# Split units through three rotating in-place buffers, one more plain unit in layer 1, and the gram matrix as two bursts of 64-row matmuls

## The chip, the cores and the metric

One core of one Trainium2 chip. The metric is the device time of one execution in microseconds (us); the median of three runs of the kernel before is 1188.52 us (1185.98 to 1189.31). Engines in the rows: PE is TensorE, PEld its weight loads, DVE is VectorE, ACT is ScalarE, POOL is GpSimd, SP is SyncE, which issues nearly all DMAs.

## The reference: what is computed

For 512 samples, 64 embeddings of 16 floats are looked up in 64 tables. Three layers of a compressed interaction network follow, then a small dense net on their sums:

```
e = stack(tbl_f[ids[:, f]])                 # 512 x 64 x 16
x = e
for W, b in ((W0, b0), (W1, b1), (W2, b2)):
    z = einsum('bhd,bfd->bhfd', x, e).reshape(B, h * f, d)
    x = einsum('oc,bcd->bod', W, z) + b     # o = 128
    outs.append(x.sum(axis=2))
h = relu(relu(concat(outs, dense) @ W_top1 + b_top1) @ W_top2 + b_top2)
y = h @ W_top3
```

All is float32. Only the sum of layer 3 over d is needed, so the kernel computes it from the gram matrix of x2 and e: gram[h, f] = sum over d of x2[h, d] e[f, d], for each sample.

## The kernel before

The batch goes through in 16 chunks of 32 samples, a chunk being 512 columns (sample, d). Partitions hold rows h. Layer 1 of a chunk is one group of 16 row tiles of z, plus one for the squares; layer 2 is four groups. A group has four units of four tiles of 128x512, at positions 0 to 3.

A unit is formed by DVE as a product of a shifted copy of e (x0_shift) and a shifted copy of x, which ScalarE copies from `land` into a PSUM bank (`to_bank`, L779). Position 0 is plain fp32 (`float_unit`, L1037): TensorE multiplies it in two passes per tile. The three others are split into two parts in fp32r, z_hi (rounded by ScalarE, `round_unit`, L803) and z_lo (z minus z_hi), and each tile takes three matmuls with the likewise split weights (`split_tile`, L1042). For positions 1 and 3 the low part is made by GpSimd (`low_part`, L525); position 2 is formed in PSUM in two halves (`form_half`, L597) and split by DVE (`split_half`, L603). z, z_hi and z_lo have three slots of their own, one for each position; DVE's next unit of a position waits for GpSimd's subtraction of the one before, ScalarE's rounding for TensorE's use of the one before.

GpSimd also issues the gathers of the chunk after next, one or two after each low part, 16 per chunk (L516). Its round has ten low parts.

For the gram of the chunk before, x2 is turned (`turn_x2`, L1097), copied out as x2t (L838), and e is turned into x0t_ps (`turn_x0`, L1088). DVE makes from it four block matrices of eight samples each (`form_block`, L638), two buffers in turn: row (sample, d), columns (sample, field), zero off the sample's own block. `gram_of` (L1106) multiplies one: 128 rows, 512 columns, fp32, into turn_gram_ps; ScalarE copies it out (`take_gram`, L844), and only then may the next start. They are spread over a chunk: after position 0 of groups 1, 2 and 3 and at the end. SyncE stores the gram of each half chunk to HBM.

The order of each engine is written out by hand in its `round_`. TensorE's round is groups 0 and 1 of layer 2, layer 1 of the next chunk, groups 2 and 3. In the tail the 16 blocks of the gram are loaded from HBM (`load_gram`, L457) and multiplied with W2 (L1168, L1178); the dense net ends the kernel.

## Time and profile before

| | |
|---|---|
| runs, median (least to most) | 1188.52 us (1185.98 to 1189.31) |
| the profiled execution's own time | 1185.75 us |
| its span in the profile | 1183.9 us |
| TensorE clock granted, mean | 0.996 |
| HBM read, written | 114.96 MB, 27.53 MB |

A row of section 5 reads: line, engine, operation, written tile <- read tiles, shapes, count; then busy us and mean ns of one; then the engine's idle time just before, and what ended it. A row of a timeline reads: start in us, length in us, engine, line, operation, count, and in brackets the idle time before it with its releaser. TensorE's matmuls overlap in the records by their latency, so the distance of two starts says what one costs.

### The profile page before, as it was taken

How to read it: one execution, taken by the hardware profiler on the slowest of the kernel's cores; microseconds unless marked ns; L12 is line 12 of the kernel's file. 1: busy time of each engine (PE TensorE's matmuls, PEld its weight loads, DVE VectorE, ACT ScalarE, POOL GpSimd, SP SyncE). 2: the span in 40 equal slices, each digit the busy share in tenths (PEclk: the TensorE clock that was granted, in tenths of full speed). 3: DMA queues.
4: the chain of work that ended last, by engine and by line, in shares of the span. 5: the costliest groups of instructions: out<-in, count | busy, mean ns of one | idle time of the engine just before them, and what ended most of it. 6: DMA issues, size and time to landing. Idle time of an engine off the chain costs nothing.

```text
span 1183.9 us, 14016 instructions
## 1 busy us (share of the span) xinstructions
PE 1121.4 (95%) x4212; PEld 758.6 (64%) x4212; DVE 1013.0 (86%) x701; ACT 714.2 (60%) x712; POOL 981.2 (83%) x419
## 2 busy tenths in 40 slices
PE   0589999999999999999999999999999999999998
PEld 0346666666766666666667666666666676667685
DVE  4598899989899999999898989999998989996542
ACT  5365566666666666666666656666666666565633
POOL 6679999999999999999999999999999997776000
PEclk9989999999999999999999999999999999999999
DMA  6641414325262515143252525251432525242991
GB/s 239 185 125 54 113 47 143 98 79 157 70 167 73 145 59 166 46 129 110 78 155 71 166 73 148 58 163 46 132 107 78 156 71 165 73 152 107 276 297 48
DMA packets 103836, 142.86 MB, mean 121 GB/s; under 512 B 11745, under 2 KB 55009, under 8 KB 103042
## 3 DMA queue, kind: packets, MB, share of 16 engines
q1 hardware_dynamic: 95618, 140.42, 39.4%
q0 software_dynamic: 8192, 2.11, 2.1%
q8 instruction: 14, 0.23, 0.1%
q14 instruction: 12, 0.10, 0.0%
HBM read 114.96 MB, written 27.53 MB: 120 GB/s over the span
## 4 chain that ended last, share of the span: by engine, by line
POOL 62%; PE 18%; issue 15%; DMA 3%; DVE 1%; ACT 1%; SPq 0%; POOLq 0%; DVEq 0%; ACTq 0%
POOL z_lo L525 46%; POOL emb L516 16%; PE acc L1042 9%; PE acc L1037 4%; DMA z<-gram_scratch 2%; PE z_ps L1178 1%; PE turn_gram_ps L1106 1%; DMA land<-x_scratch 1%; PE z_ps L1168 1%; ACT z_hi L1004 0%; DVE z_lo L768 0%; DVE z L591 0%; PE turn_gram_ps L1210 0%; PE x0t_ps L1210 0%; DMA x_scratch<-emb 0%
## 5 line engine op out<-in xcount | busy, mean ns | idle before, releaser
L525 POOL TENSOR_TENSOR z_lo<-z,z_hi 128x2048 fp32r<-128x2048 f32 x159 | 735.1, 4623 | 47.2 <-ACT z_hi L803 44.6
L803 ACT ACTIVATE z_hi<-z 128x2048 fp32r<-128x2048 f32 x160 | 306.2, 1914 | 180.6 <-PE acc L1042 169.3
L1042 PE MATMUL acc<-z_hi,w_hi 128*128 128x512 f32 x960 | 412.2, 429 | 2.6 <-POOL z_lo L525 2.3
L1042 PE MATMUL acc<-z_hi,w_lo 128*128 128x512 f32 x960 | 378.8, 395 | 0.0
L1042 PE MATMUL acc<-z_lo,w_hi 128*128 128x512 f32 x960 | 378.8, 395 | 0.0
L591 DVE TENSOR_TENSOR z<-operand_even,x_shift 128x2048 f32<-128x2048 f32 x144 | 328.7, 2283 | 21.3 <-POOL z_lo L525 7.0
L516 POOL DMA_INDIRECT emb<-in_tables,rows_chunk x256 | 245.9, 961 | 61.9 <-issue 56.7
L1037 PE MATMUL acc<-z,w_sb 128*128 128x512 f32 x640 | 294.1, 603 | 0.5 <-ACT x L832 0.4
L603 DVE TENSOR_TENSOR z_lo<-z_ps,z_hi 128x1024 fp32r<-128x1024 f32 x160 | 194.8, 1218 | 72.3 <-ACT z_hi L812 72.3
L1042 PEld LDWEIGHTS acc<-z_hi,w_hi 128*128 128x128 f32 x960 | 180.7, 188 | 62.1 <-issue 18.4
L591 DVE TENSOR_TENSOR z<-operand_odd,x_shift 128x2048 f32<-128x2048 f32 x96 | 219.0, 2281 | 0.7 <-POOL z_lo L525 0.3
L1042 PEld LDWEIGHTS acc<-z_lo,w_hi 128*128 128x128 f32 x960 | 180.9, 188 | 57.2 <-issue 18.9
L1037 PEld LDWEIGHTS acc<-z,w_sb 128*128 128x128 f32 x640 | 121.6, 192 | 143.4 <-issue 127.2
L1042 PEld LDWEIGHTS acc<-z_hi,w_lo 128*128 128x128 f32 x960 | 180.7, 188 | 42.5
L812 ACT ACTIVATE z_hi<-z_ps 128x1024 fp32r<-128x1024 f32 x160 | 165.2, 1032 | 59.9 <-DVE z_ps L597 59.6
L597 DVE TENSOR_TENSOR z_ps<-operand_odd,x_shift 128x1024 f32<-128x1024 f32 x128 | 157.2, 1228 | 2.2
L779 ACT ACTIVATE operand_even<-land 128x512 f32<-128x512 f32 x96 | 57.4, 598 | 88.6 <-DMA land<-x_scratch 50.2
L844 ACT ACTIVATE gram<-turn_gram_ps 128x512 f32<-128x512 f32 x64 | 68.6, 1071 | 58.9 <-PE turn_gram_ps L1106 54.1
L1106 PE MATMUL turn_gram_ps<-blocks,x2t 128*128 128x512 f32 x128 | 67.8, 611 | 5.4 <-DVE blocks L638 5.3
L1065 PE MATMUL acc<-z_sq,w_sb 64*128 64x512 f32 x32 | 19.8, 701 | 47.1 <-ACT z_sq L818 39.9
L779 ACT ACTIVATE operand_odd<-land 128x512 f32<-128x512 f32 x96 | 57.2, 596 | 8.2 <-DMA land<-x_scratch 6.0
L638 DVE TENSOR_TENSOR blocks<-x0t_ps,mask_sb 128x512 f32<-128x512 f32 x64 | 43.6, 681 | 8.9 <-PE x0t_ps L1088 8.1
(106 smaller groups left out, 468.4 us busy)
## 6 DMA issues: line engine op xcount, KB each, us to landing
land<-x_scratch SPq DMA_DIRECT2D x128, 256.0 KB
land<-x_scratch SPq DMA_DIRECT2D x128, 128.0 KB
x_shift<-x_scratch SPq DMA_DIRECT2D x16, 1024.0 KB, 5.9
gram_scratch<-gram SPq DMA_DIRECT2D x32, 512.0 KB, 4.4
x_shift<-x_scratch SPq DMA_DIRECT2D x16, 768.0 KB, 8.0
z<-gram_scratch SPq DMA_DIRECT2D x10, 1024.0 KB, 10.8
x_scratch<-emb SPq DMA_DIRECT2D x32, 192.0 KB, 2.9
x_shift<-gram_scratch SPq DMA_DIRECT2D x6, 1024.0 KB, 10.5
```

The lines of the kernel that those rows point to most:

```text
L516: pool.indirect_dma_start(out=emb[:, c.par, j * EMBED:(j + 1) * EMBED], out_offset=None, in_=tables, in_offset=bass.IndirectOffsetOnAxis(a ...
L525: pool.tensor_tensor(z_lo[:, slot], z[:, Z_SLOT[pos]], z_hi[:, slot].bitcast(F32), ALU.subtract).then_inc(subtracted, 1)
L591: dve.tensor_tensor(z[:, Z_SLOT[pos]], *times(bank, QUAD, x0_tiles), ALU.mult).then_inc(formed, 1)
L597: dve.tensor_tensor(z_ps[:, :, :], *times(bank, 2, x0_tiles), ALU.mult).then_inc(halves_formed, 1)
L603: dve.tensor_tensor(z_lo[:, SPLIT_SLOT[2], tiles], z_ps[:, :, :], z_hi[:, SPLIT_SLOT[2], tiles].bitcast(F32), ALU.subtract).then_inc(halve ...
L779: act.activation(operand[bank][:, :], land[:, slot, :], ACT.Copy).then_inc(copied, 1)
L803: act.activation(z_hi[:, SPLIT_SLOT[pos]], z[:, Z_SLOT[pos]], ACT.Copy).then_inc(rounded, 1)
L812: act.activation(z_hi[:, SPLIT_SLOT[2], 2 * half:2 * half + 2], z_ps[:, :, :], ACT.Copy).then_inc(halves_rounded, 1)
L844: act.activation(gram[:, :, b % 2 * GROUP_B:(b % 2 + 1) * GROUP_B].rearrange("p f b -> p b f"), turn_gram_ps[:, :].rearrange("p (b f) -> p ...
L1037: mm = pe.matmul(acc[:, :], weights[:, tile0 + q, :], z[:, Z_SLOT[0], q, :], start=start and q == 0, stop=False)
L1042: mm = pe.matmul(acc[:, :], w[:, tile, :], zz[:, slot, q, :], start=False, stop=stop and n == 2)
L1106: pe.matmul(turn_gram_ps[:, :], x2t[:, b * P:(b + 1) * P], blocks[:, b % 2].rearrange("p b f -> p (b f)"), start=True, stop=True).then_inc ...
```

## The change

- Split units of positions 1 and 3 rotate through three buffers, z_hi slot and z_lo slot together; z lies in z_lo's memory, and GpSimd subtracts in place. Plain units rotate through two buffers z_float. `Group` gets functions that tell a unit's slot and which use of TensorE frees it; DVE's forming waits for that use. ScalarE's rounding waits for the formed unit alone.
- Layer 1's position 3 is a plain fp32 unit: no rounding, no low part; its weights move to w0_sb. GpSimd's round has nine low parts.
- The gram of a chunk is taken in two halves of two 128-row blocks. A block is two matmuls of 64 rows and 256 columns, one on partitions 0 to 63 into turn_gram_ps, one on 64 to 127 into x0t_ps's bank. The halves stand after position 0 of groups 1 and 2. One DVE instruction forms all blocks (128x1024), before the middle of group 1. ScalarE copies out both banks after each half, at other places of its round, the last after the rounding of the next chunk's first unit; TensorE waits for all four copies before the last unit of a chunk.
- The third piece of W2 is loaded two units later. The scratch for GpSimd's DMA descriptors is set to 8192.

The diff, cut to its core:

```diff
+HALF_ROWS = P // 2
+TILE_B = HALF_ROWS // EMBED
+HALVES, BANK_BLOCKS = 2, BLOCKS // 2
+GRAM_BANKS = 2
...
-L1_SPLIT = SPLIT_UNITS * QUAD
+L1_SPLIT = 2 * QUAD
 L2_SPLIT = L2_GROUPS * SPLIT_UNITS * QUAD
 SPLIT_TILES = L1_SPLIT + L2_SPLIT
-L1_PLAIN, L2_PLAIN = QUAD, L2_GROUPS * QUAD
-Z_SLOT = {0: 0, 1: 1, 3: 2}
-SPLIT_SLOT = {1: 0, 3: 1, 2: 2}
+L1_PLAIN, L2_PLAIN = 2 * QUAD, L2_GROUPS * QUAD
+FLOAT_SLOTS, UNIT_SLOTS = 2, 3
+HALVES_SLOT = UNIT_SLOTS
...
+    def layer1_at(self, back):
+        j = self.j - back
+        return j in (-1, 0) if self.chunk.is_(0) else self.has_layer1 and j == 2
+    def before(self):
+        if self.chunk.is_(0):
+            return 1 + self.j, min(1 + self.j, 2)
+        return 1 + self.j, 1 + (self.has_layer1 and self.j > 2)
+    def units(self, more=0):
+        groups, layer1 = self.before()
+        return self.chunk.count(2 * GROUPS - 1, 2 * groups - layer1 + more)
+    def unit_slot(self, pos):
+        groups, layer1 = self.before()
+        return (2 * groups - layer1 + pos // 3) % UNIT_SLOTS
+    def float_slot(self, pos):
+        groups, layer1 = self.before()
+        return (groups + layer1 + pos // 3) % FLOAT_SLOTS
+    def unit_freed(self, pos):
+        past = [(0, 1)] if pos == 3 else []
+        for back in range(1, 4):
+            past += [(back, 1)] if self.layer1_at(back) else [(back, 3), (back, 1)]
+        back, at = past[UNIT_SLOTS - 1]
+        return self.freed(back, at)
+    def float_freed(self, pos):
+        past = [(0, 0)] if pos == 3 else []
+        for back in range(1, 4):
+            past += [(back, 3), (back, 0)] if self.layer1_at(back) else [(back, 0)]
+        back, at = past[FLOAT_SLOTS - 1]
+        return self.freed(back, at)
+    def freed(self, back, at):
+        if self.chunk.is_(0) and self.j - back < -1:
+            return None
+        return self.count(QUAD, at + 1 - QUAD * back)
...
-        z = sb("z", [P, len(Z_SLOT), QUAD, COLS])
-        z_hi = sb("z_hi", [P, len(SPLIT_SLOT), QUAD, COLS], F32R)
-        z_lo, z_lo_whole = sb_twice("z_lo", "z_lo_whole", [P, len(SPLIT_SLOT), QUAD, COLS])
+        z_float = sb("z_float", [P, FLOAT_SLOTS, QUAD, COLS])
+        z_hi = sb("z_hi", [P, UNIT_SLOTS + 1, QUAD, COLS], F32R)
+        z_lo, z = sb_twice("z_lo", "z", [P, UNIT_SLOTS + 1, QUAD, COLS])
...
-        blocks = sb("blocks", [P, 2, GROUP_B, FIELDS])
+        blocks = sb("blocks", [P, BLOCKS, TILE_B, FIELDS])
...
+        gram_banks = [turn_gram_ps[:, :], x0t_ps[:, :, :].rearrange("p b f -> p (b f)")]
...
-            load_w2(3, 3)
+            load_w2(3, 3, units_used=2)
...
-                slot = SPLIT_SLOT[pos]
-                pool.wait_ge(rounded, g.count(2, (pos + 1) // 2))
-                pool.tensor_tensor(z_lo[:, slot], z[:, Z_SLOT[pos]], z_hi[:, slot].bitcast(F32),
+                slot = g.unit_slot(pos)
+                pool.wait_ge(rounded, g.units((pos + 1) // 2))
+                pool.tensor_tensor(z_lo[:, slot], z[:, slot], z_hi[:, slot].bitcast(F32),
                                    ALU.subtract).then_inc(subtracted, 1)
             def round_(c, look_up=True, groups=GROUPS):
                 done = 0
                 for j in range(groups):
                     for pos in (1, 3):
-                        low_part(Group(c, j), pos)
+                        if not (pos == 3 and Group(c, j).is_layer1):
+                            low_part(Group(c, j), pos)
...
-                if not g.is_first:
-                    if pos == 0:
-                        dve.wait_ge(used, g.count(4, -3))
-                    else:
-                        dve.wait_ge(subtracted, g.count(2, -2 + (pos + 1) // 2))
-                dve.tensor_tensor(z[:, Z_SLOT[pos]], *times(bank, QUAD, x0_tiles), ALU.mult).then_inc(formed, 1)
+                is_float = pos == 0 or pos == 3 and g.is_layer1
+                freed = g.float_freed(pos) if is_float else g.unit_freed(pos)
+                if freed is not None:
+                    dve.wait_ge(used, freed)
+                out = z_float[:, g.float_slot(pos)] if is_float else z[:, g.unit_slot(pos)]
+                dve.tensor_tensor(out, *times(bank, QUAD, x0_tiles), ALU.mult).then_inc(formed, 1)
...
-            def form_block(c, b):
-                if b == 0:
-                    dve.wait_ge(x0_turned, c.count(1, 1))
-                if not (c.is_(0) and b < 2):
-                    dve.wait_ge(gram_done, c.count(BLOCKS, b - 1))
+            def form_blocks(c):
+                dve.wait_ge(x0_turned, c.count(1, 1))
+                if not c.is_(0):
+                    dve.wait_ge(gram_done, c.count(HALVES))
+                shape = [P, BLOCKS, TILE_B, FIELDS]
                 dve.tensor_tensor(
-                    blocks[:, b % 2], x0t_ps[:, b:b + 1, :].to_broadcast([P, GROUP_B, FIELDS]),
-                    mask_sb[:, :].rearrange("p (b f) -> p b f", f=1).to_broadcast([P, GROUP_B, FIELDS]),
+                    blocks[:, :, :, :],
+                    x0t_ps[:, 0:BLOCKS, :].rearrange("p (k o) f -> p k o f", o=1).to_broadcast(shape),
+                    mask_sb[:, :].rearrange("p (k b f) -> p k b f", k=1, f=1).to_broadcast(shape),
                     ALU.mult).then_inc(block_ready, 1)
...
                 layer2(c, 1, 0)
+                form_blocks(prev)
                 layer2_middle(c, 1)
-                form_block(prev, 0)
                 layer1(nxt, 1)
                 split_half(layer2_group(c, 1), 1)
                 sum2(prev)
                 layer1(nxt, 0)
-                form_block(prev, 1)
                 layer1_middle(nxt)
-                form_block(prev, 2)
                 layer2(c, 2, 1)
...
             def round_unit(g, pos):
                 act.wait_ge(formed, g.count(3, pos))
-                if not g.is_first:
-                    act.wait_ge(used, g.count(4, pos - 3))
-                act.activation(z_hi[:, SPLIT_SLOT[pos]], z[:, Z_SLOT[pos]], ACT.Copy).then_inc(rounded, 1)
+                act.activation(z_hi[:, g.unit_slot(pos)], z[:, g.unit_slot(pos)], ACT.Copy).then_inc(rounded, 1)
...
-            def take_gram(c, b):
-                act.wait_ge(gram_done, c.count(BLOCKS, b + 1))
-                if b % 2 == 0 and not (c.is_(0) and b == 0):
-                    act.wait_ge(gram_stored, c.count(32, 16 * (b // 2)))
-                act.activation(gram[:, :, b % 2 * GROUP_B:(b % 2 + 1) * GROUP_B].rearrange("p f b -> p b f"),
-                               turn_gram_ps[:, :].rearrange("p (b f) -> p b f", f=FIELDS), ACT.Copy).then_inc(gram_staged, 1)
+            def take_gram(c, half, bank):
+                act.wait_ge(gram_done, c.count(HALVES, half + 1))
+                if bank == 0 and not (c.is_(0) and half == 0):
+                    act.wait_ge(gram_stored, c.count(32, 16 * half))
+                act.activation(gram[:, :, :].rearrange("p f (k r b) -> p r k b f", k=BANK_BLOCKS, r=GRAM_BANKS)[:, bank],
+                               gram_banks[bank].rearrange("p (k b f) -> p k b f", k=BANK_BLOCKS, f=FIELDS),
+                               ACT.Copy).then_inc(gram_staged, 1)
...
-                take_gram(prev, 2)
+                take_gram(prev, 1, 0)
                 round_half(e, 1)
                 to_bank(f, 1, 1, released_by_layer2(e, 1))
                 round_unit(f, 1)
+                take_gram(prev, 1, 1)
...
-            def float_unit(g, acc, weights, tile0, start=False):
-                pe.wait_ge(formed, g.count(3, 2))
+            def float_unit(g, acc, weights, tile0, pos=0, start=False, stop=False):
+                pe.wait_ge(formed, g.count(3, 2 if pos == 0 else 3))
                 for q in range(QUAD):
-                    mm = pe.matmul(acc[:, :], weights[:, tile0 + q, :], z[:, Z_SLOT[0], q, :], start=start and q == 0, stop=False)
+                    mm = pe.matmul(acc[:, :], weights[:, tile0 + q, :], z_float[:, g.float_slot(pos), q, :],
+                                   start=start and q == 0, stop=stop and q == QUAD - 1)
                 mm.then_inc(used, 1)
...
-                split_unit(g, 3, acc1, 2 * QUAD, stop=True)
+                float_unit(g, acc1, w0_sb, QUAD, pos=3, stop=True)
...
-                            pe.wait_ge(block_ready, c.count(BLOCKS))
+                            pe.wait_ge(gram_staged, c.count(BLOCKS))
...
-            def gram_of(c, b):
-                if b == 0:
+            def gram_of(c, half):
+                if half == 0:
                     pe.wait_ge(x2t_ready, c.count(1, 1))
+                    pe.wait_ge(block_ready, c.count(1, 1))
                 else:
-                    pe.wait_ge(gram_staged, c.count(BLOCKS, b))
-                pe.wait_ge(block_ready, c.count(BLOCKS, b + 1))
-                pe.matmul(turn_gram_ps[:, :], x2t[:, b * P:(b + 1) * P],
-                          blocks[:, b % 2].rearrange("p b f -> p (b f)"), start=True, stop=True).then_inc(gram_done, 1)
+                    pe.wait_ge(gram_staged, c.count(BLOCKS, GRAM_BANKS))
+                for k in range(BANK_BLOCKS):
+                    b = half * BANK_BLOCKS + k
+                    for r in range(GRAM_BANKS):
+                        rows = slice(r * HALF_ROWS, (r + 1) * HALF_ROWS)
+                        mm = pe.matmul(gram_banks[r][:, k * TILE_B * FIELDS:(k + 1) * TILE_B * FIELDS],
+                                       x2t[rows, b * P:(b + 1) * P],
+                                       blocks[rows, b].rearrange("p b f -> p (b f)"), start=True, stop=True)
+                mm.then_inc(gram_done, 1)
...
-                layer2(c, 3, (0,))
-                gram_of(prev, 2)
-                layer2(c, 3, (1, 2, 3))
+                layer2(c, 3, range(QUAD))
                 turn_x0(c)
-                gram_of(prev, 3)
...
-        "mask": (np.arange(P)[:, None] // EMBED == np.arange(GROUP_B)[None, :]).astype(np.float32),
+        "mask": (np.arange(P)[:, None] % HALF_ROWS // EMBED == np.arange(TILE_B)[None, :]).astype(np.float32),
...
-    nc = bacc.Bacc("TRN2", target_bir_lowering=False, num_devices=1)
+    nc = bacc.Bacc("TRN2", target_bir_lowering=False, num_devices=1, dynamic_dma_scratch_size=8192)
```

In ScalarE's round the other three copies stand after `round_unit(d, 1)`, after `take_x1(nxt)` and after `round_unit(e, 3)`.

## Rows read from the trace of the kernel before

**Rows 1.** The page, engines: busy us, share of the span, instructions.

```profile
PE 1121.4 (95%) x4212; PEld 758.6 (64%) x4212; DVE 1013.0 (86%) x701; ACT 714.2 (60%) x712; POOL 981.2 (83%) x419
```

**Rows 2.** The chain that ended last: shares by engine, then by line.

```profile
POOL 62%; PE 18%; issue 15%; DMA 3%; DVE 1%; ACT 1%; SPq 0%; POOLq 0%; DVEq 0%; ACTq 0%
POOL z_lo L525 46%; POOL emb L516 16%; PE acc L1042 9%; PE acc L1037 4%; DMA z<-gram_scratch 2%; PE z_ps L1178 1%; PE turn_gram_ps L1106 1%; DMA land<-x_scratch 1%; PE z_ps L1168 1%; ACT z_hi L1004 0%; DVE z_lo L768 0%; DVE z L591 0%; PE turn_gram_ps L1210 0%; PE x0t_ps L1210 0%; DMA x_scratch<-emb 0%
```

**Rows 3.** The chain piece by piece (start, us), and GpSimd's groups of section 5.

```profile
463.00 4.64 POOL z_lo L525
...
528.17 4.64 POOL z_lo L525
...
L525 POOL TENSOR_TENSOR z_lo<-z,z_hi 128x2048 fp32r<-128x2048 f32 x159 | 735.1, 4623 | 47.2 <-ACT z_hi L803 44.6
...
L516 POOL DMA_INDIRECT emb<-in_tables,rows_chunk x256 | 245.9, 961 | 61.9 <-issue 56.7
```

**Rows 4.** Waits from 131 to 910 us: us, times, longest.

```profile
PE turn_gram_ps L1106 <- DVE blocks L638: 4.7, 6, 1.4
...
POOL z_lo L525 <- ACT z_hi L803: 1.1, 2, 0.9
```

**Rows 5.** Timeline of ScalarE: start, us; one copy of x2 per chunk (chunks 0, 12, 13, 14).

```profile
131.30 0.69 ACT L832 ACTIVATE x<-acc,bias_sb 128x512 f32<-128x512 f32 x1 [2.22 <-PE acc L1042]
...
914.61 0.69 ACT L832 ACTIVATE x<-acc,bias_sb 128x512 f32<-128x512 f32 x1 [0.59 <-PE acc L1042]
...
980.20 0.69 ACT L832 ACTIVATE x<-acc,bias_sb 128x512 f32<-128x512 f32 x1 [0.67 <-PE acc L1042]
...
1044.93 0.69 ACT L832 ACTIVATE x<-acc,bias_sb 128x512 f32<-128x512 f32 x1 [0.74 <-PE acc L1042]
```

**Rows 6.** Busy us (and instructions) of each engine in a stretch, granted clock, DMA.

```profile
329.10:393.70 64.60, 64.60 (x239) 43.64 (x239) 59.87 (x42) 41.43 (x41) 61.00 (x27) 1.00 0.38 108
```

**Rows 7.** Timeline of TensorE in a steady chunk, and a unit from the chain.

```profile
485.04 0.39 PE L1042 MATMUL acc<-z_hi,w_lo 128*128 128x512 f32 x1
485.37 1.12 PE L1065 MATMUL acc<-z_sq,w_sb 64*128 64x512 f32 x2
486.42 3.70 PE L1037 MATMUL acc<-z,w_sb 128*128 128x512 f32 x8
...
498.35 3.59 PE L1037 MATMUL acc<-z,w_sb 128*128 128x512 f32 x8
501.79 1.02 PE L1106 MATMUL turn_gram_ps<-blocks,x2t 128*128 128x512 f32 x2
...
985.04 2.79 PE acc L1042 x12
```

**Rows 8.** Groups of section 5: DVE's block instruction and one of 1024 elements.

```profile
L597 DVE TENSOR_TENSOR z_ps<-operand_odd,x_shift 128x1024 f32<-128x1024 f32 x128 | 157.2, 1228 | 2.2
...
L638 DVE TENSOR_TENSOR blocks<-x0t_ps,mask_sb 128x512 f32<-128x512 f32 x64 | 43.6, 681 | 8.9 <-PE x0t_ps L1088 8.1
```

**Rows 9.** DVE, ScalarE's gram copy and TensorE about the end of a chunk.

```profile
514.45 2.28 DVE L591 TENSOR_TENSOR z<-operand_even,x_shift 128x2048 f32<-128x2048 f32 x1
...
L844 ACT ACTIVATE gram<-turn_gram_ps 128x512 f32<-128x512 f32 x64 | 68.6, 1071 | 58.9 <-PE turn_gram_ps L1106 54.1
...
520.87 0.39 PE L1042 MATMUL acc<-z_hi,w_hi 128*128 128x512 f32 x1
```

**Rows 10.** Timeline of TensorE at the start.

```profile
64.94 2.04 PE L1065 MATMUL acc<-z_sq,w_sb 64*128 64x512 f32 x2 [7.18 <-ACT x L825]
...
80.94 3.59 PE L1037 MATMUL acc<-z,w_sb 128*128 128x512 f32 x8
```

**Rows 11.** Tail: DMA issues on SyncE's queue, and ScalarE's last rounding of gram.

```profile
1087.30 0.43 SPq L474 DMA_DIRECT2D w_whole<-in_w  x1
...
1096.66 0.38 SPq L457 DMA_DIRECT2D z<-gram_scratch  x1
...
1161.08 1.91 ACT L1004 ACTIVATE z_hi<-z 128x2048 fp32r<-128x2048 f32 x1 [1.54 <-DMA z<-gram_scratch]
```

More of the change, by code:

```diff
@@ L129, in __init__ @@
         self.is_first = chunk.is_(0) and j == -1
+        self.has_layer1 = not chunk.is_(CHUNKS - 1)
+        self.is_layer1 = self.layer1_at(0)
     def count(self, per_group, more=0):
         return self.chunk.count(GROUPS * per_group, per_group * (1 + self.j) + more)
+    def layer1_at(self, back):
[30 more added lines that the diff above has]
+        return self.count(QUAD, at + 1 - QUAD * back)
     def copies(self, more=0):
@@ L232, in gram_view @@
             return b.rearrange("p q (h n) -> p (q h) n", h=CHUNKS // QUAD).rearrange("p c (f b) -> p c f b", f=F_BLOCK)
-        gram_buffers = [gram_view(b) for b in (z[:, 0], z[:, 1], z[:, 2], x0_shift[:, 1, 0:QUAD], x0_shift[:, 1, QUAD:])]
+        gram_buffers = [gram_view(b) for b in (z_float[:, 0], z_float[:, 1], z[:, HALVES_SLOT], x0_shift[:, 1, 0:QUAD], x0_shift[:, 1, QUAD:])]
         GRAM_BUFFERS = len(gram_buffers)
-        gram_hi, gram_lo = ([gram_view(b[:, slot]) for slot in range(len(SPLIT_SLOT))] for b in (z_hi, z_lo))
+        gram_hi, gram_lo = ([gram_view(b[:, slot]) for slot in range(UNIT_SLOTS)] for b in (z_hi, z_lo))
         GRAM_SLOTS = len(gram_hi)
         wt2_sb = land[:, 0:2, :].rearrange("p a (h n) -> p (a h) n", h=2)
-        h1, h2, y_sb = z[:, 2], z_lo_whole[:, 2], z_sq[0:1, :]
+        h1, h2, y_sb = z_float[:, 0], z_float[:, 1], z_sq[0:1, :]
         acc1 = ps("acc1", [P, COLS])
@@ L469, in reload_gram, with load_w2 @@
                 load_gram(k)
-            def load_w2(part, groups_used):
-                sp.wait_ge(used, Group(end, groups_used).count(4))
+            def load_w2(part, groups_used, units_used=0):
+                sp.wait_ge(used, Group(end, groups_used).count(4, units_used))
                 sp.dma_start(w2_parts[part], w2[:, part * W2_PART:(part + 1) * W2_PART, :]).then_inc(w2_in[part], 16)
@@ L542, in _ @@
                 gather(c, range(HALF_B))
-            low_part(layer1_group(Chunk(0, 0)), 3)
-            with pool.Fori(0, (CHUNKS - 2) // 2) as n:
-                round_(Chunk(n, 0))
-                round_(Chunk(n, 1))
+            round_(Chunk(0, 0))
+            round_(Chunk(0, 1))
+            with pool.Fori(0, (CHUNKS - 4) // 2) as n:
+                round_(Chunk(n, 2))
+                round_(Chunk(n, 3))
             round_(Chunk(0, CHUNKS - 2), look_up=False)
@@ L602, in split_half @@
                 tiles = slice(2 * half, 2 * half + 2)
-                dve.tensor_tensor(z_lo[:, SPLIT_SLOT[2], tiles], z_ps[:, :, :],
-                                  z_hi[:, SPLIT_SLOT[2], tiles].bitcast(F32), ALU.subtract).then_inc(halves_split, 1)
+                dve.tensor_tensor(z_lo[:, HALVES_SLOT, tiles], z_ps[:, :, :],
+                                  z_hi[:, HALVES_SLOT, tiles].bitcast(F32), ALU.subtract).then_inc(halves_split, 1)
             def layer1(c, pos, half=None):
@@ L759, in _ @@
             split_w2(1)
-            form_block(end, 2)
             split_w2(2)
-            form_block(end, 3)
             split_w2(3)
@@ L1045, in split_unit @@
             def split_unit(g, pos, acc, tile0, stop=False):
-                pe.wait_ge(subtracted, g.count(2, (pos + 1) // 2))
+                pe.wait_ge(subtracted, g.units((pos + 1) // 2))
                 for q in range(QUAD):
-                    mm = split_tile(acc, tile0 + q, SPLIT_SLOT[pos], q, stop and q == QUAD - 1)
+                    mm = split_tile(acc, tile0 + q, g.unit_slot(pos), q, stop and q == QUAD - 1)
                 mm.then_inc(used, 1)
```

61 lines of the change are left out of this document (24 added, 37 removed).

## Prediction

> **What bounds the kernel now.** The page comes first. TensorE (PE) is busy 95% of the span, GpSimd (POOL) 83%, VectorE (DVE) 86% [rows 1]: three engines near full, so shares decide nothing. The chain of waits says which ends last: 62% of it is POOL, two thirds of that z_lo, the subtraction that splits a unit, and PE is only 18% [rows 2]. The pieces of the chain in order of time show a round of POOL: z_lo starts at 463.00 and the same one of the next chunk at 528.17, 65.17 us later [rows 3]. It holds 10 z_lo at 4.62 us and 16 gathers at 0.96, together 61.6 us, and 3.6 us of gaps. From 131 to 910 us POOL waited for a rounded unit 1.1 us in all [rows 4]: it is full.
>
> How fast does the whole go? ScalarE's L832 takes x2 once per chunk. From 131.30 to 914.61 lie 12 chunks, so 65.28 us each, POOL's round and 0.1 [rows 5]. Later, 980.20 to 1044.93, POOL gathers no more and a chunk takes 64.73 us [rows 5]. One earlier chunk took 64.6, with PE busy 64.60 of 64.60 [rows 6]. So PE's own floor is 64.6, only 0.6 below POOL. Relief of POOL alone can't pay more than that; what the change does to PE decides.
>
> PE's floor from its own rows: 12 split matmuls, a unit, take 2.79 us, 0.2325 each; a plain fp32 unit (8 passes) is 498.35 to 501.79, 3.43 us; a gram block (2 passes) 0.86 us [rows 7]. 15 split units 41.9, 5 plain 17.2, 4 gram blocks 3.4, the squares with what surrounds them 1.15 (below): 63.6, and the two turns are the other 1.0.
>
> **The change part by part.** *Layer 1's fourth unit in plain fp32.* On POOL one z_lo of ten goes: 65.2 − 4.6 = 60.6 us a round. On ScalarE a rounding of 1.9 us goes, off the path (busy 41 of 65 us [rows 6]). On PE 12 split matmuls become 8 fp32 passes: 3.43 − 2.79 = +0.64 us a chunk, all on the path once PE bounds.
>
> *The gram on PE.* Four blocks, each 2 passes of 512 columns, become 8 matmuls of 64 rows and 256 columns, in two bursts of four. No row shows a pass of 256 fp32 columns over 64 rows; half of the 0.429 us pass is 0.2145. A burst has 8 such passes. Run one by one they take 1.72 us; wholly overlapped in pairs 0.86. In between: the two passes of one matmul use the same 64 rows and the same bank, so they can't overlap each other, and the queue holds them in order, pass 1 and 2 of the upper rows, then of the lower. Overlap then comes only between the second pass of one and the first of the next: slots A1, A2+B1, B2+C1, C2+D1, D2, five of 0.2145, 1.07 us. I take 1.07.
> Going over to 64 rows and back costs too: the squares are such a matmul. The last split one ends its slot at 485.04 + 0.23 = 485.27, the squares start at 485.37, use 0.86 and would be done at 486.23, the next unit starts at 486.42 [rows 7]: 0.10 + 0.19 = 0.29 us, for each burst.
> So a chunk's gram is 2 × (1.07 + 0.29) = 2.72 instead of 3.43: −0.71. Wholly overlapped 2.30 (−1.13), one by one 4.02 (+0.59).
> The Trainium skill (TensorEngine Tiling (Array Packing), Key Properties) says that tiles work in parallel, but that changing the tiling mode drains TensorE; the 0.29 us of the squares agrees with the drain. It also gives up to 2× for 64 rows; no run here shows that, and by a full 2× the gram would save 1.13 us a chunk, by none it would cost 0.59.
>
> *One block-matrix instruction on DVE.* Four of 0.68 us go [rows 8]. The new one writes 128x1024 from PSUM; the nearest is L597, also 1024 elements per partition, 1.23 us; upper end 4 × 0.68 = 2.72. I take 1.23. DVE's chunk is 59.9 us busy [rows 6], becomes about 59, and stays under PE. PE's wait for a block (4.7 us in all [rows 4]) goes: the instruction now comes ahead of the middle of group 1, while PE has 3.43 us of the plain unit to do. It hides itself.
>
> *Three in-place buffers.* DVE's form no longer waits for POOL's subtraction but for PE's use three units back, and ScalarE's rounding not for PE at all, which is off the path. Place by PE's clock, group start = 0, units at 0, 3.43, 6.22, 9.01, next group 11.8. Position 3 may be formed when position 1 of the group before is used, at −5.6; form 2.28, round 1.91, subtract 4.62 end at +3.3, needed at 9.01: 5.7 us to spare, about one more z_lo with a gather. Position 1 may be formed at −11.8 and has 6.4 to spare. Cost 0; without that cover PE waits by what is lacking. The subtraction in place has the same shape; I count it 0, and as POOL has 4 us of spare it could be 0.4 us dearer each before it bounds.
>
> *The moved waits.* x0t's bank now holds half of the gram, so PE's last split unit of a chunk (before turn_x0) waits for all four copies out, the last being after ScalarE's rounding of the next chunk's first unit. Queued behind that wait: PE's whole stream. By before's rows: the next chunk's first unit is formed at 514.45 + 2.28 = 516.73, rounded in 1.91 and the copy takes 1.07: 519.7. PE comes to its last unit at 520.87 [rows 9]: 1.2 us to spare, 0 on the path. Four copies of 1.07 us remain four.
>
> *Start.* PE's layer 1 of chunk 1 starts at 64.94, after a 7.18 wait [rows 10]: it comes from the 32 gathers and the loads behind them, which stay. From there to 131.30 [rows 5] are 66.3 us; floor of four layer 2 groups is 4 × 11.8, layer 1 took 16.0, to 80.94 [rows 10], together 63.2, so POOL costs 3.0 here, and 2 of its subtractions go: −3.0 + 0.64 = −2.4. The smaller descriptor scratch could make gathers wait: no row shows one that waited for its ring, the mean of all 256 is 0.96 [rows 3]; I take 0 and at most 3 us, as many in the start as make three of them twice as long.
>
> *Tail.* From 1098 on DMA bounds: 16 loads of gram (and 3 stores) fill the 63 us up to 1161, where the last rounding waits for its load [rows 11], and PE and ScalarE wait for them. Fewer PE steps there gain nothing. The third piece of W2 is loaded after two more units, about 1091 instead of 1087.30, still ahead of the first gram load at 1096.66 [rows 11]: 0, at most +3 if they collide.
>
> **Sum.** Period: 64.6 + 0.64 − 0.71 = 64.5, with 0.1 for small waits, as 64.73 stands to 64.6: 64.65. The 14 intervals from 131.30 to 1044.93 are 913.6; after 905.1: −8.5. Chunk 0: −2.4. Last interval, without layer 1: −0.7. Tail 0. Together −11.6: the span 1183.9 becomes 1172.3, the execution 1185.75 becomes 1174.1. The median of the runs shown is 1188.52, 2.8 above that execution; against it I predict 1177.
>
> **The rivals.**
> *Whole overlap (1171).* Pairs run side by side in both passes: 0.42 less a chunk, over 15 chunks −6 us. For: two banks, two row halves. Against: the order of the passes above.
> The Trainium skill (TensorE: Matmul & The Clock Gate, Measured speedup vs the span model) has 3.07 from four 32-row tiles, not 4; two at that efficiency would lie near this or the forecast.
> *No overlap (1196), the other side.* 64-row passes queue up. A chunk is 64.6 + 0.64 + 0.59 = 65.8, 0.55 over today and 1.3 over the forecast: +1.3 × 15 = 19 us. For: no row shows two matmuls at once, and in every row a pass starts a full slot after the last. Against: all these use the same rows of the array. It decides from a burst of about 1.4 us on: there the gram and the plain unit cost what POOL's relief gives.
> *PE doesn't reach its floor (1186).* The chain form, round, subtract is tied to PE's pace now, and POOL at 60.6 of 64.6 is 94% full; handovers keep the period near 65.2 while only the start gains. 14 × 0.6 over the forecast. For: today every chunk but some sits 0.7 above PE's floor. Against: 5.7 us of cover, and the chunk at 64.73 with similar chains.
> *The wait for four copies bites (1194).* If DVE is only just ahead of PE, the 1.2 us of cover goes and PE pays about 1.1 a chunk.
>
> **How the numbers follow.** Forecast 0.45, whole overlap 0.15, no overlap 0.17, floor missed 0.15, copies or gathers 0.08. What a measurement can tell from no change is 0.3%, 3.6 us. Faster: the first two and a quarter of the third kind, 0.64; same 0.12 (the floor missed); slower 0.24. The forecast's own range is 1171 to 1183. For 8 in 10: down to 1168, whole overlap with some of the switching hidden, up to 1194, so that only the no-overlap case stays out.
>
> **What would show it.** z_lo count 143 instead of 159 and POOL waiting for roundings in the middle; L832 64.5 to 64.8 apart; from float unit to split unit around a burst 1.36 us (1.15 with whole overlap, 2.0 with none); one blocks row of 1.23 us; no idle of PE ahead of a chunk's last split unit. Wrong it is if the burst is 1.7 or more, or if PE has idle stretches of a microsecond in each chunk.

## The result, and the profile after

The changed kernel takes 1183.31 us (median of 6 runs, 1182.75 to 1183.81); the kernel before took 1187.99 (6 runs, 1185.98 to 1189.31) beside it. The ratio of the times, after over before, is 0.9965 with a 95% interval of [0.9954, 0.9975]: faster by 4.2 us by the ratio and 4.7 by the two medians, where 11.6 were forecast. (Ratios here and below are those on record; they can differ from the quotient of the medians shown in the fourth place.) The profiled execution went from 1185.75 to 1183.49 us, its span from 1183.9 to 1181.5.

The page after answers to [rows 1 to 3] and [rows 8]. First the engines' busy time; then the chain that ended last, by engine and by line; then groups as line, engine, operation, tiles, count, busy us, mean ns, idle before and releaser.

```profile
PE 1117.9 (95%) x4276; PEld 745.3 (63%) x4276; DVE 997.4 (84%) x652; ACT 681.9 (58%) x695; POOL 905.2 (77%) x403
...
PE 83%; POOL 4%; issue 3%; DMA 3%; SPq 2%; ACT 2%; DVE 1%; ACTq 0%
...
L580 POOL TENSOR_TENSOR z_lo<-z,z_hi 128x2048 fp32r<-128x2048 f32 x143 | 659.5, 4613 | 116.8 <-ACT z_hi L849 110.3
L1079 PE MATMUL acc<-z_float,w_sb 128*128 128x512 f32 x768 | 349.1, 601 | 8.2 <-ACT x L878 7.6
```

GpSimd has left the chain (62% to 4%), TensorE is it (18% to 83%): the bound moved as the prediction had it. The subtraction costs no more in place: 4613 ns against 4623. The waits of the steady part, 131 to 910 us, answer to [rows 4]:

```profile
POOL z_lo L580 <- ACT z_hi L849: 46.0, 42, 2.5
...
PE acc L1079 <- ACT x L878: 6.3, 12, 0.6
```

GpSimd now waits 46 us instead of 1.1, and TensorE's granted clock is 1.00 in this stretch in both kernels, so the clock plays no part there. The last row is new: once in each chunk TensorE's first plain unit waits for ScalarE's copy of x2. It looks small. The timeline of TensorE shows what it is part of; start and length in us, the bracket is the idle time before:

```profile
500.99 0.48 PE L1153 MATMUL turn_gram_ps<-blocks,x2t 64*128 64x256 f32 x1
501.00 0.48 PE L1153 MATMUL x0t_ps<-blocks,x2t 64*128 64x256 f32 x1
501.31 0.38 PE L1153 MATMUL turn_gram_ps<-blocks,x2t 64*128 64x256 f32 x1
501.32 0.38 PE L1153 MATMUL x0t_ps<-blocks,x2t 64*128 64x256 f32 x1
...
501.75 0.38 PE L1153 MATMUL turn_gram_ps<-blocks,x2t 64*128 64x256 f32 x1
501.75 0.38 PE L1153 MATMUL x0t_ps<-blocks,x2t 64*128 64x256 f32 x1
502.06 0.50 PE L1085 MATMUL acc<-z_hi,w_hi 128*128 128x512 f32 x1
...
522.09 0.39 PE L1085 MATMUL acc<-z_hi,w_lo 128*128 128x512 f32 x1
522.41 0.46 PE L1131 MATMUL x0t_ps<-ident_sb,x_shift 64*128 64x64 f32 x4
523.34 3.69 PE L1079 MATMUL acc<-z_float,w_sb 128*128 128x512 f32 x8 [0.46 <-ACT x L878]
```

The same place in the kernel before, from its timeline:

```profile
523.42 0.40 PE L1042 MATMUL acc<-z_hi,w_lo 128*128 128x512 f32 x1
523.75 0.46 PE L1088 MATMUL x0t_ps<-ident_sb,x_shift 64*128 64x64 f32 x4
524.15 1.12 PE L1106 MATMUL turn_gram_ps<-blocks,x2t 128*128 128x512 f32 x2
525.11 3.60 PE L1037 MATMUL acc<-z,w_sb 128*128 128x512 f32 x8
```

The next plain unit reuses the bank of x2, so it can't start until ScalarE has copied x2 out, which needs the last split matmul to end. Before, turn and gram block filled that time: from the block's end (524.15 + 0.86 = 525.01) the unit starts 0.1 later. The turn alone leaves a hole. The slot of a matmul is the distance from its start to the next one's in an unbroken row, 0.23 us for a split one. The slot of the last split matmul ends at 522.09 + 0.23 = 522.32, the plain unit starts at 523.34, 1.02 later, and its record is 0.1 longer (3.69 against 3.60): 1.12 in all. Before, that stretch without the gram block was 525.11 − 0.86 − (523.42 + 0.23) = 0.60. So 0.52 us of every chunk came back.

The burst itself beat the forecast. In both passes the two halves start 0.01 us apart. A pair comes each 0.21 us, four pairs are 0.86, and 0.40 is lost going in and out (0.09 before the first pair, 0.10 more than a slot from the first pair to the second, 0.10 behind the last, 0.10 more than a slot from the first split matmul to the second): 1.26 us against 1.36 forecast, 2.52 a chunk against 3.43 before. The gram gave −0.91, not −0.71.

ScalarE's copies of x2 give the pace (chunks 0, 12, 13, 14, 15), as [rows 5]:

```profile
132.23 0.69 ACT L878 ACTIVATE x<-acc,bias_sb 128x512 f32<-128x512 f32 x1 [4.04 <-PE acc L1085]
...
912.90 0.69 ACT L878 ACTIVATE x<-acc,bias_sb 128x512 f32<-128x512 f32 x1 [3.16 <-PE acc L1085]
977.90 0.69 ACT L878 ACTIVATE x<-acc,bias_sb 128x512 f32<-128x512 f32 x1 [3.10 <-PE acc L1085]
1042.83 0.69 ACT L878 ACTIVATE x<-acc,bias_sb 128x512 f32<-128x512 f32 x1 [3.10 <-PE acc L1085]
1094.08 0.69 ACT L878 ACTIVATE x<-acc,bias_sb 128x512 f32<-128x512 f32 x1 [10.37 <-PE acc L1085]
```

Between the two profiled executions the span balances: the first copy came 0.9 us later, the 14 intervals shrank from 913.6 to 910.6 (−3.0), the last one from 51.7 to 51.25 (−0.4), what lies behind it grew by 0.1: −2.4. That the medians differ by 4.7 is more than that, because the profiled execution of the kernel before was 2.2 us quicker than its median; what its other executions spend there no trace shows.

### The profile page after: what moved, and what is told of

The parts are those of the page before. It is cut to its first block, busy times and chain, and to the rows that moved or that the text cites. A ratio compares the mean times of both kernels' runs of the same rounds, so it can differ in the third digit from the quotient of the medians.

```text
span 1181.5 us, 13928 instructions
## 1 busy us (share of the span) xinstructions
PE 1117.9 (95%) x4276; PEld 745.3 (63%) x4276; DVE 997.4 (84%) x652; ACT 681.9 (58%) x695; POOL 905.2 (77%) x403
## 4 chain that ended last, share of the span: by engine, by line
PE 83%; POOL 4%; issue 3%; DMA 3%; SPq 2%; ACT 2%; DVE 1%; ACTq 0%
PE acc L1085 50%; PE acc L1079 26%; POOL z_lo L580 3%; PE turn_gram_ps L1153 3%; DMA z_float<-gram_scratch 2%; PE acc L1108 1%; POOL emb L571 1%; ACT x L878 1%; DMA z<-gram_scratch 1%; PE z_ps L1214 1%; PE turn_gram_ps L1140 1%; DMA land<-x_scratch 1%; ACT z_hi L1046 0%; DVE z_lo L816 0%; SPq L512 0%
## 5 line engine op out<-in xcount | busy, mean ns | idle before, releaser
L580 POOL TENSOR_TENSOR z_lo<-z,z_hi 128x2048 fp32r<-128x2048 f32 x143 | 659.5, 4613 | 116.8 <-ACT z_hi L849 110.3
L1085 PE MATMUL acc<-z_hi,w_hi 128*128 128x512 f32 x896 | 379.0, 423 | 6.8 <-DVE z_lo L659 4.2
L1079 PE MATMUL acc<-z_float,w_sb 128*128 128x512 f32 x768 | 349.1, 601 | 8.2 <-ACT x L878 7.6
L1085 PE MATMUL acc<-z_lo,w_hi 128*128 128x512 f32 x896 | 354.3, 395 | 0.0
L849 ACT ACTIVATE z_hi<-z 128x2048 fp32r<-128x2048 f32 x144 | 275.1, 1910 | 53.6 <-DVE z L647 53.6
L1079 PEld LDWEIGHTS acc<-z_float,w_sb 128*128 128x128 f32 x768 | 144.4, 191 | 174.6 <-issue 166.4
L647 DVE TENSOR_TENSOR z<-operand_even,x_shift 128x2048 f32<-128x2048 f32 x80 | 183.0, 2287 | 37.3 <-PE acc L1085 16.6
L647 DVE TENSOR_TENSOR z_float<-operand_even,x_shift 128x2048 f32<-128x2048 f32 x64 | 146.1, 2283 | 10.2 <-PE acc L1079 8.6
L647 DVE TENSOR_TENSOR z<-operand_odd,x_shift 128x2048 f32<-128x2048 f32 x64 | 146.2, 2284 | 4.3 <-PE acc L1085 4.3
L647 DVE TENSOR_TENSOR z_float<-operand_odd,x_shift 128x2048 f32<-128x2048 f32 x32 | 73.0, 2282 | 5.0 <-ACT operand_odd L827 5.0
```

What stands on the lines that cost most here:

```text
L580: pool.tensor_tensor(z_lo[:, slot], z[:, slot], z_hi[:, slot].bitcast(F32), ALU.subtract).then_inc(subtracted, 1)
L647: dve.tensor_tensor(out, *times(bank, QUAD, x0_tiles), ALU.mult).then_inc(formed, 1)
L849: act.activation(z_hi[:, g.unit_slot(pos)], z[:, g.unit_slot(pos)], ACT.Copy).then_inc(rounded, 1)
L1079: mm = pe.matmul(acc[:, :], weights[:, tile0 + q, :], z_float[:, g.float_slot(pos), q, :], start=start and q == 0, stop=stop and q == QUAD ...
L1085: mm = pe.matmul(acc[:, :], w[:, tile, :], zz[:, slot, q, :], start=False, stop=stop and n == 2)
```

## The experiments

The theory put to test: the gram's gain is real and whole; TensorE is the bound; the removed gram block had covered the copy of x2. Each variant's time is set against the kernel before on its own chip; a copy of x2 per chunk gives the pace.

**e1: is the wait slack?** The turn of e is issued twice, more work in the hole.

```diff
-                turn_x0(c)
+                turn_x0(c, times=2)
```

> The changed kernel with turn_x0's four transposes issued twice, so that TensorE has 0.4 us more work between the last split unit of a chunk and the next chunk's plain unit. Theory (there TensorE waits about 0.5 us for ScalarE's copy of x2, which the last gram matmul used to cover): the transposes fill the wait, the distance of two x2 copies stays within 0.1 us of 65.04 and the time within 2 us of 1183.3. Rival (the whole of TensorE's work sets the time, the wait is a product of how the records are read): 16 times 0.4 us more, about 1189.5.

Ratio 0.9964 [0.9950, 0.9978], 1182.01 us against 1185.86. Four matmuls more per chunk cost nothing, the copies of x2 stay 65.05 us apart (65.04):

```profile
519.33 0.71 PE L1131 MATMUL x0t_ps<-ident_sb,x_shift 64*128 64x64 f32 x8
520.25 3.69 PE L1079 MATMUL acc<-z_float,w_sb 128*128 128x512 f32 x8 [0.21 <-ACT x L878]
```

The matmuls run longer (0.71 against 0.46) and the idle time shrinks by the same 0.25. The hole is there and its end is set by ScalarE.

**e2: fill the hole with work that must be done anyway.** The second burst goes to the end of the chunk, the turn of e behind the turn of x2 in the next; ScalarE's copies of that half move with them.

```diff
-                layer2(c, 2, (0,))
-                gram_of(prev, 1)
-                layer2(c, 2, (1, 2, 3))
+                layer2(c, 2, range(QUAD))
                 layer2(c, 3, range(QUAD))
-                turn_x0(c)
+                gram_of(prev, 1)
```

> The changed kernel with its second gram burst moved from position 0 of group 2 to the end of the chunk, turn_x0 moved behind turn_x2 of the next round, and ScalarE's copies moved accordingly (its rounding of position 3 ahead of the copy of x2). Theory (uncovered x2 copy): a burst of 1.26 us now covers the 1.02 us from the last matmul to x2's release; the end of a chunk and both turns cost 0.5 us less, the x2 copies come 64.5 us apart, the time is 8 us under the changed kernel, about 1175.5. Rival (another unit is late as soon as this wait goes: GpSimd at 60.6 us a round or DVE near 59 with handovers): no gain, 1182 to 1185, with PE waiting for z_lo or formed units.

1175.1 us, ratio 0.9907 [0.9892, 0.9922]. Copies of x2 from 129.99 to 1032.85 over 14 intervals, 64.49 apart against 65.04: −0.55, the 0.52 of the hole. From 131 to 910 us TensorE's wait for the copy is nearly gone, one case where the changed kernel had twelve (6.3 us):

```profile
PE acc L1081 <- ACT x L878: 0.8, 1, 0.8
```

The theory holds. Against the changed kernel's profile the span is 6.5 us shorter: −7.7 from the 14 intervals, −2.2 from a first copy that comes earlier (the start, e3 and e11, which this edit doesn't touch), and +3.3 from the last interval, 54.58 instead of 51.25 (e10).

**e3: is the smaller descriptor scratch the cause of the late start?** The kernel before with it alone.

```diff
-    nc = bacc.Bacc("TRN2", target_bir_lowering=False, num_devices=1)
+    nc = bacc.Bacc("TRN2", target_bir_lowering=False, num_devices=1, dynamic_dma_scratch_size=8192)
```

> The kernel before with one edit, the descriptor scratch at 8192. Theory (the start's 3 us come from the smaller scratch, which slows the issue of DMAs): layer 1 of chunk 1 begins about 2 us later, near 67, the time is 2 us up. Rival (the start is later for another reason, such as where weights land): starts at 64.9, time unchanged within 0.5 us.

1185.15 us, ratio 0.9995 [0.9986, 1.0004]; layer 1 of chunk 1 starts at 65.66 (64.94 before, 67.06 after), and SyncE's loads are issued as early as in the kernel before (by 41.1 us; e11). The smaller scratch alone doesn't make the late issue, and e6 has the late issue without it.

**e4: does the overlap need the two halves as neighbours in the queue?** All matmuls of the upper rows first, then those of the lower.

```diff
-                for k in range(BANK_BLOCKS):
-                    b = half * BANK_BLOCKS + k
-                    for r in range(GRAM_BANKS):
+                for r in range(GRAM_BANKS):
+                    for k in range(BANK_BLOCKS):
+                        b = half * BANK_BLOCKS + k
```

> The changed kernel with the four matmuls of a gram burst in another order: both blocks of partitions 0 to 63 first, then both of 64 to 127, instead of alternating. Theory (neighbours overlap only if they sit on different rows, and an fp32 matmul issues both passes as one, so only the second and third can overlap): a burst goes from 1.26 to about 1.7 us (three slots of 0.43 and 0.40 of switching), 0.43 twice a chunk, 15 chunks: +13 us, 1196. Rival (the queue looks past the neighbour and overlaps all four anyway): no change, 1183. Without any overlap it would be 2.1 us a burst and 1209.

1182.09 us, ratio 0.9967 [0.9954, 0.9980]: no difference. That part of the theory fell.

```profile
498.80 0.48 PE L1153 MATMUL turn_gram_ps<-blocks,x2t 64*128 64x256 f32 x1
498.81 0.48 PE L1153 MATMUL x0t_ps<-blocks,x2t 64*128 64x256 f32 x1
499.12 0.38 PE L1153 MATMUL turn_gram_ps<-blocks,x2t 64*128 64x256 f32 x1
499.13 0.38 PE L1153 MATMUL x0t_ps<-blocks,x2t 64*128 64x256 f32 x1
...
499.87 0.50 PE L1085 MATMUL acc<-z_hi,w_hi 128*128 128x512 f32 x1
```

From the first pair to the split matmul it is 1.07 us, as in the changed kernel. The second half starts beside the first although four passes of the first stand ahead of it.

**e5 and e6: which part brings the gain?** e5 is the change with the old gram, e6 the kernel before with the new gram alone, so that its buffers, its descriptor scratch and its ten subtractions are those of before. One core of each edit:

```diff
 e5, against the changed kernel
-                form_blocks(prev)
+                form_block(prev, 0)
...
-                gram_of(prev, 1)
+                gram_of(prev, 3)
 e6, against the changed kernel
-                        if not (pos == 3 and Group(c, j).is_layer1):
-                            low_part(Group(c, j), pos)
+                        low_part(Group(c, j), pos)
```

> The change without its gram: rotating in-place buffers, fourth unit of layer 1 in plain fp32, but the gram in four blocks of 128 rows as before, one of them again at the end of a chunk. My theory: what the change gains in the steady part is the gram on TensorE alone, and GpSimd's relief is worth nothing without it, since the plain unit adds 0.64 us a chunk to TensorE's 64.6. ScalarE's copies of x2 then stand 65.2 to 65.4 us apart, TensorE is the bound, and the time is that of the kernel before less what the start gains: 1184.5 to 1187 against 1185.9. Rival: the buffers and GpSimd's relief bring the gain and the gram little: 1178 to 1182, copies 64.9 apart or less.

> The kernel before with the gram of the change alone (two bursts of 64-row matmuls, one block instruction, the moved copies), with ten subtractions a round on GpSimd. My theory: GpSimd's round of 65.2 us still ends last, TensorE merely idles more, so copies of x2 stand 65.1 to 65.3 apart and the time is 1184 to 1187 against 1185.9. Rival: TensorE was the real bound of the kernel before, and its 0.92 less 0.52 us a chunk shows: 1178 to 1181, copies 64.9 apart.

e5: 1189.7 us against 1187.66, ratio 1.0018 [1.0009, 1.0027]; GpSimd's relief with the dearer plain unit makes the kernel slower by 2 us. That is 0.9 us above my range. The 14 intervals are 65.55 on average; the first and the third are long (66.7 and 67.0), the later ones 65.36, 0.12 over the sum of 65.24. What makes these differences wasn't traced. e6: 1185.53, ratio 0.9984 [0.9975, 0.9994], 1.9 us faster, copies 65.09 apart. Their chains, by engine, e5:

```profile
PE 82%; issue 5%; POOL 4%; DMA 3%; DVE 3%; SPq 2%; ACT 1%; DVEq 0%; ACTq 0%
```

and e6:

```profile
POOL 66%; issue 16%; PE 10%; DMA 3%; DVE 3%; ACT 1%; SPq 1%; POOLq 0%; ACTq 0%; DVEq 0%
```

With relief and buffers alone TensorE bounds at once and pays for the plain unit; with the gram alone GpSimd goes on bounding. Neither rival stands. But the parts are not equal: the gram alone already brings 1.9 us, and in the steady chunks most of what the change gained (65.09 us against 65.04 in the changed kernel and 65.26 before). The relief adds 0.05 us a chunk to that, because with the hole TensorE bounds at once, and about a microsecond in chunk 0: from layer 1's start to the copy of x2 it is 65.2 us with it (changed kernel, e5) and 66.3 without (kernel before, e6). It pays more once the hole is filled: e2's 64.49 lies below GpSimd's round with ten subtractions, 65.1. Buffers and the fourth plain unit were not tried one without the other.

**e7: share the way in and out.** e2 with the first burst directly before layer 1's squares, also a matmul of 64 rows.

```diff
-                layer2(c, 1, (0,))
+                layer2(c, 1, range(QUAD))
                 gram_of(prev, 0)
-                layer2(c, 1, (1, 2, 3))
```

> The moved version (second burst at the end of the chunk, turn of e behind the turn of x2) with the first burst put directly before layer 1's squares, which are 64-row matmuls too. My theory: a burst costs 0.86 us of passes and 0.40 of going over to 64 rows and back; beside the squares one such going over is shared, 0.29 to 0.40 us a chunk in 14 chunks: 4 to 5.5 us less than the 1175.1 of the moved version, 1169.5 to 1171.5, and copies of x2 64.1 to 64.2 apart. Rival: the 0.40 is latency of the burst's own matmuls, not of the change of shape, and nothing is shared: 1175, copies 64.5 apart.

1174.44 us, ratio 0.9891 [0.9876, 0.9906].

```profile
542.11 0.40 PE L1087 MATMUL acc<-z_hi,w_lo 128*128 128x512 f32 x1
542.43 0.48 PE L1153 MATMUL turn_gram_ps<-blocks,x2t 64*128 64x256 f32 x1
...
543.40 1.02 PE L1110 MATMUL acc<-z_sq,w_sb 64*128 64x512 f32 x2
544.35 2.84 PE L1081 MATMUL acc<-z_float,w_sb 128*128 128x512 f32 x6
```

From the split matmul's end, 542.34, to the plain unit 2.01 us for burst and squares; apart they took 1.16 (502.06 in the changed kernel less the end of the plain unit at 500.90) and 1.15 us. That saves 0.30, and the 0.10 by which the first slot behind such a matmul is longer is paid once less. The pace confirms the sum: 64.09 against 64.49. The 0.40 us is a cost of the change of shape. Yet the time missed the expected 1169.5 to 1171.5; it fell by less than the 5.6 us of 14 such intervals: the first copy came 2.2 us later (132.22 against 129.99, with the late issue of e11) and the last interval grew by 1.0, to 55.58.

**e8: GpSimd in chunk 0.** e7 with eight gathers of the first round ahead of layer 2.

```diff
+                            upto = max(done, upto, early * (1 + pos // 2) // 2)
...
-            round_(Chunk(0, 0))
+            round_(Chunk(0, 0), early=8)
```

> The version before with GpSimd's gathers of its first round put ahead: eight of the sixteen during layer 1 of chunks 0 and 1, when it waits for 3.4 us, so that fewer stand between its subtractions of chunk 0's layer 2. My theory: GpSimd bounds that stretch (12.5 us a group against TensorE's 11.8), so the copy of x2 of chunk 0 comes 1.0 to 1.5 us earlier, and the time is 1 to 1.5 us below the version before. Rival: another wait bounds chunk 0: no change, or 1 to 2 us worse, since eight gathers delay the first subtractions of layer 2.

1171.76 us, ratio 0.9866 [0.9851, 0.9881], 2.7 less than e7. From layer 1's start to the copy of x2 64.30 us (65.86 to 130.16) against 65.18 in e7 (67.04 to 132.22): −0.9, just under my range. e10, with the same gathers, has 63.52 (67.45 to 130.97), −1.7; all variants of the changed kernel without them have 65.1 to 65.3, whenever layer 1 starts. So the gathers cost 0.9 to 1.7 us here. The rest of e8's gain, 1.2 us, is an earlier start of layer 1, which the edit doesn't explain.

**e9: is it the rows?** Both matmuls of a block on the same 64 rows.

```diff
-                        rows = slice(r * HALF_ROWS, (r + 1) * HALF_ROWS)
+                        rows = slice(0, HALF_ROWS)
```

> The changed kernel with both matmuls of a gram block on partitions 0 to 63 (the part of the gram on partitions 64 to 127 is replaced by the upper part twice). Counts, shapes and banks are the same. My theory: the pairs of a burst overlap because they use different rows of the array. On the same rows the eight passes run one by one, 1.72 us instead of 0.86: a burst takes 2.1 us instead of 1.26, a chunk 1.7 more, and the time is 1183.3 plus 24 to 27: 1206 to 1210, copies of x2 66.7 to 66.9 apart. Rival: 64-row passes of 256 columns are just cheaper, or overlap in any case: no change.

1207.42 us against 1185.35, ratio 1.0185 [1.0168, 1.0202], copies 66.79 apart.

```profile
508.58 0.70 PE L1153 MATMUL turn_gram_ps<-blocks,x2t 64*128 64x256 f32 x2
509.12 0.59 PE L1153 MATMUL x0t_ps<-blocks,x2t 64*128 64x256 f32 x2
509.55 0.59 PE L1153 MATMUL turn_gram_ps<-blocks,x2t 64*128 64x256 f32 x2
509.98 0.59 PE L1153 MATMUL x0t_ps<-blocks,x2t 64*128 64x256 f32 x2
510.50 0.50 PE L1085 MATMUL acc<-z_hi,w_hi 128*128 128x512 f32 x1
```

Now two passes of one matmul are one row, and a row takes 0.43 us (the first 0.54): 1.92 from the first to the split unit against 1.07. This is the prediction's rival of no overlap. Its ratio lies 0.022 above the changed kernel's, some 26 us: without the overlap the change would be a loss.

**e10: the last chunk.** e8 with SyncE's loads ahead of its wait for the turn of e, which the move of e2 had made later.

```diff
+            for i in range(4, SHIFTS - 1):
+                load_shift(end, i)
             sp.wait_ge(halves_formed, Group(end.plus(-1), 4).count(2, 2))
             sp.wait_ge(x0_turned, CHUNKS - 1)
```

> The version with early gathers, and in SyncE's queue of the last chunk the loads of shifted x1 put ahead of the wait for the turn of e, which that version has 8 us later in the chunk. My theory: ScalarE stood 9.33 us for such a load at 1044.76 and the last interval of the copies of x2 was 55.6 us against 51.7 in the kernel before, only because SyncE waited with the loads queued behind. The last interval becomes 51 to 52 us, and the time 3.5 to 4.5 us less than 1171.8: 1167 to 1168.5. Rival: the last chunk is held up by something else of the moved order: 55 us and 1171 to 1172.

1168.35 us against 1187.36, ratio 0.9837 [0.9818, 0.9855], the best of all. ScalarE's copies of x2 of the last two chunks:

```profile
1028.29 0.69 ACT L879 ACTIVATE x<-acc,bias_sb 128x512 f32<-128x512 f32 x1 [3.12 <-PE acc L1088]
...
1079.12 0.69 ACT L879 ACTIVATE x<-acc,bias_sb 128x512 f32<-128x512 f32 x1 [9.04 <-PE acc L1088]
```

The interval is 50.8 us; in e8 it was 55.6. The cause was the one foreseen: a step moved on TensorE held a wait on SyncE, with loads queued behind.

**e11: is the late start the kernel's?** The changed kernel once more, with no edit.

> The changed kernel once more, nothing edited, for its start. Its first profile has layer 1 of chunk 1 at 67.06 us on TensorE where the kernel before has 64.94, and SyncE issuing its loads later from 32 to 50 us. If this comes from the kernel (its length of code, its order of addresses), it is at 67.0 again; if from the execution or the chip, it can be at 64.8, as in most variants. The time lies at 1181 to 1184 in both cases.

1182.91 us, ratio 0.9962 [0.9951, 0.9972], and layer 1 of chunk 1 at 67.46. So the late start goes with the kernel, as far as two profiled executions can tell. Its issues on SyncE's queue in this run:

```profile
31.85 0.69 SPq L383 DMA_DIRECT2D x_shift<-x_scratch  x1
34.68 6.38 SPq L417 DMA_DIRECT2D land<-x_scratch  x4
43.85 3.50 SPq L383 DMA_DIRECT2D x_shift<-x_scratch  x2
48.79 1.42 SPq L417 DMA_DIRECT2D land<-x_scratch  x2
```

and in e2, with the same code for this part:

```profile
31.76 0.51 SPq L383 DMA_DIRECT2D x_shift<-x_scratch  x1
32.38 2.38 SPq L417 DMA_DIRECT2D land<-x_scratch  x4
34.86 1.07 SPq L383 DMA_DIRECT2D x_shift<-x_scratch  x2
39.92 1.11 SPq L417 DMA_DIRECT2D land<-x_scratch  x2
```

The same nine loads are all issued by 50.2 us instead of 41.0, and no wait is named for the stretches between. Both ran on the same chip. The changed kernel, e6, e7 and e10 have it, e5 and e8 in part, the kernel before, e1, e2, e3, e4 and e9 not; e1 and the changed kernel differ in nothing that runs by then. Layer 1 of chunk 1 starts at 66.1 to 67.5 us in the four that have it and at 63.9 to 65.7 in those without. What it is stays open, and every comparison of two variants by their whole time carries these 1 to 3 us; the paces don't.

## Why the prediction was off

*The bound and its floor: right.* TensorE took over, GpSimd waits, no chunk waits for buffers. The rival "TensorE doesn't reach its floor" falls with e2, e7 and e10: without the hole the chunks run at 64.49 and 64.09.

*The plain unit, +0.64: right.* e5, which has it without the new gram, runs at 65.36 in its later chunks against the 64.6 floor + 0.64.

*The burst: mis-sized, in the kernel's favour.* −0.91 instead of −0.71 a chunk. The step that failed is "the queue holds them in order": it made the halves overlap in five slots instead of four. They overlap wholly, even when queued by rows (e4), and only where the rows differ (e9). That the two passes of one matmul don't overlap holds (e9). The halves went to two banks in every run, so whether one bank would do is not shown. The way in and out is 0.40, not 0.29: what was read from the squares left out that the first slot of the next shape is 0.10 longer. The Trainium skill (TensorEngine Tiling (Array Packing), Key Properties) says that a change of tiling mode drains TensorE; the 0.40 us lost at each burst agrees. The Trainium skill (TensorEngine Tiling (Array Packing), Theoretical Speedup) gives up to 2× where a dimension is 64 or less; the trace agrees, and the 2× is whole: 0.86 us for passes that e9 shows to take 1.72 one by one. So the mechanism of the rival "whole overlap" is what happened, but not its 1171 us.

*The moved waits: the step that failed most.* The prediction checked the wait that the change adds (TensorE for four copies; no idle time ahead of the last split unit, right) and the work that moved, but put the move of the fourth gram block away from the end of the chunk at nothing, without asking what it did there. The listing shows it: behind the turn and this block comes a unit that starts a new sum in the very bank that the copy of [rows 5] has yet to read. Price 0.52 a chunk (e2 gets 0.55 back): +7.3 us over the 14 intervals. With the better burst (−2.8) and a rest of 0.07 that no row names (+1.0) the period is 65.04 instead of 64.65, and −8.5 became −3.0. Of the prediction's signs, its pace of 64.5 to 64.8 warned of this; the idle record of 0.46 us alone stayed below the microsecond that it had named.

*The start: −2.4 forecast, +0.9 measured.* One part is the late issue on SyncE (+2.1 at layer 1 of chunk 1). From there to the copy of x2 it is 65.2 us instead of 66.4, −1.2. The prediction had let two subtractions go and then counted TensorE's floor; but GpSimd still bounds chunk 0 (e8). Its timeline after:

```profile
71.12 0.96 POOL L571 DMA_INDIRECT emb<-in_tables,rows_chunk  x1 [0.16 <-issue]
...
79.26 4.54 POOL L580 TENSOR_TENSOR z_lo<-z,z_hi 128x2048 fp32r<-128x2048 f32 x1 [3.43 <-ACT z_hi L849]
...
130.21 4.60 POOL L580 TENSOR_TENSOR z_lo<-z,z_hi 128x2048 fp32r<-128x2048 f32 x1
```

It idles 3.4 us before the four groups of layer 2, which have no layer 1 between them here: eight subtractions and twelve gathers from 79.26 to 130.21, 12.7 us a group against TensorE's 11.8 (e8's expectation says 12.5). A round's mean says nothing about its densest part.

*Blocks, tail, buffers: right.* DVE's instruction takes 1216 ns on average (1.23 forecast) and TensorE never waits for it; behind the last copy of x2 lie 87.4 us (87.3).

```profile
529.88 1.22 DVE L694 TENSOR_TENSOR blocks<-x0t_ps,mask_sb 128x1024 f32<-128x1024 f32 x1
```

In sum, the profiled pair was to lose 11.6 us and lost 2.4: 5.5 too little in the steady chunks, 3.3 at the start, 0.3 in the last interval, 0.1 behind it. That the median, 1183.31, still comes out just beyond the upper end of the forecast's range and not further off is partly luck: the burst's error covered part of the hole's, and the 2.8 us that the prediction added to get from the profiled execution to a median were not there in the changed kernel (0.2 less).

## What to carry to other kernels

When a change takes work off an engine that is about to become the bound, ask of each removed instruction what wait it covered at its place; its cost is saved only where nothing was hidden behind it, and the cheap cure is to move other due work there (here 0.55 us a chunk, more than the 0.2 that the change itself gained in the steady chunks). Two matmuls of 64 rows on different halves of the array are worth placing in bursts, next to other work of the same shape. A step moved on one engine must be followed through the queues that wait for it, to the last turn of the loop.
